# Moving the zero-point/scale table work and the weight-rebuild halves to other slots of an attention + GPTQ feed-forward kernel

## What is computed

```python
xn = layernorm(x)
# attention: 32 heads of 32, 8 key/value heads, rope, causal softmax
s = softmax(mask(q @ k.T / sqrt(32))) @ v @ wo
# feed-forward with 4-bit weights in groups of 128 rows
w_gu[i, f] = scale_gu[g[i], f] * (nibble_gu[i, f] - (zero_gu[g[i], f] + 1))     # 1024 x 5504
h = silu(xn @ w_gu[:, :2752]) * (xn @ w_gu[:, 2752:])
w_d[f, n] = scale_d[g[f], n] * (nibble_d[f, n] - (zero_d[g[f], n] + 1))         # 2752 x 1024
out = x + s * silu(h @ w_d)
```

## Time and profile before

| | us |
|---|---|
| median of 3 runs | 2474.61 (2474.33 to 2475.61) |
| the profiled execution | 2473.97 |
| its span, first to last instruction | 2472.2 |
| attention steps of the span | about 355 to 1550 |
| PE busy | 2338.2 (95%) |
| DVE busy | 1315.3 (53%) |
| POOL busy | 1162.1 (47%) |
| ACT busy | 890.5 (36%) |

### The profile page before, as it was taken

How to read it: one execution, slowest core, us unless ns; L and a number is a source line. 1 busy time by engine, 2 the same in 40 slices (tenths; PEclk the granted TensorE clock), 3 DMA queues, 4 the chain that set the end, 5 groups by cost and what they waited for, 6 DMA issues and landing times. The chain is left out here.

```text
span 2472.2 us, 41329 instructions
## 1 busy us (share of the span) xinstructions
PE 2338.2 (95%) x16296; PEld 1190.3 (48%) x16296; DVE 1315.3 (53%) x2164; ACT 890.5 (36%) x1665; POOL 1162.1 (47%) x1260
## 2 busy tenths in 40 slices
PE   6899969999999999999999999999969999999999
PEld 3555525555555555555555555444434444444443
DVE  4687467677777677777767775456331111111100
ACT  3222125555556555556555556222210101010100
POOL 2554327777777777777777777333201000101000
PEclk9999969999999999999999999999989999999999
DMA  5332301122221222221222212233182213222120
GB/s 162 99 94 67 86 18 39 45 74 52 68 63 55 60 55 70 68 59 54 66 52 68 69 47 56 75 102 93 48 306 95 77 62 109 84 87 99 55 80 17
DMA packets 229106, 187.62 MB, mean 76 GB/s; under 512 B 121617, under 2 KB 200954, under 8 KB 228544
## 3 DMA queue, kind: packets, MB, share of 16 engines
q1 hardware_dynamic: 228928, 185.21, 25.4%
HBM read 113.17 MB, written 71.86 MB: 75 GB/s over the span
## 5 line engine op out<-in xcount | busy, mean ns | idle before, releaser
L1046 PE MATMUL gu_ps<-xT,wg 128*128 128x512 f16 x4128 | 998.8, 382 | 1.7 <-ACT h L1119 1.7
L1292 POOL TENSOR_TENSOR room<-room 128x1152 f16<-128x1152 f32 x256 | 539.8, 2108 | 65.4 <-ACT room L1078 63.2
L1046 PEld LDWEIGHTS gu_ps<-xT,wg 128*128 128x128 f16 x4128 | 370.1, 98 | 390.7 <-issue 15.4
L1078 ACT ACTIVATE room<-sc_ps 128x512 f32<-128x512 f32 (+3 forms) x768 | 349.4, 489 | 512.8 <-PE sc_ps L971 511.9
L1683 POOL TENSOR_TENSOR room<-room 128x512 f32<-128x512 f32 x32 | 52.8, 1654 | 617.5 <-DVE room L1644 617.5
L1498 PE MATMUL dn_ps<-xT,hT_in 128*128 128x512 f16 x1536 | 337.2, 380 | 0.0
L1166 DVE TENSOR_REDUCE shift<-mx_ps 128x2 f16<-128x1024 f32 (+2 forms) x252 | 208.9, 829 | 147.9 <-PE mx_ps L953 143.9
L1644 DVE TENSOR_TENSOR room<-room 128x512 f32<-128x512 f32 x32 | 24.0, 754 | 428.6 <-ACT room L1572 428.6
L1287 POOL TENSOR_SCALAR_AFFINE_SELECT room<-room 128x128 f32<-128x128 f32 x512 | 153.0, 304 | 183.4 <-ACT room L1078 179.2
L1498 PEld LDWEIGHTS dn_ps<-xT,hT_in 128*128 128x128 f16 x1536 | 148.7, 98 | 181.6 <-issue 7.5
L949 PE MATMUL mx_ps<-arena 96*128 96x512 f16 x756 | 191.4, 335 | 38.8 <-DVE part L1166 33.4
(11 more groups left out here) (120 smaller groups left out, 3000.1 us busy)
## 6 DMA issues: line engine op xcount, KB each, us to landing
hidden_scratch<-hT SPq DMA_DIRECT2D x84, 256.0 KB, 3.0
hT_in<-hidden_scratch SPq DMA_DIRECT2D x16, 1344.0 KB, 5.9
o_scratch<-room SPq DMA_DIRECT2D x16, 1040.0 KB, 6.1
room<-o_scratch SPq DMA_DIRECT2D x16, 1040.0 KB, 8.2
arena<-q_scratch SPq DMA_DIRECT2D x48, 256.0 KB, 3.7
stock<-in_qw_d SPq DMA_DIRECT2D x42, 256.0 KB
down_scratch<-wd SPq DMA_DIRECT2D x84, 128.0 KB, 2.8
xin<-in_x SPq DMA_DIRECT2D x16, 512.0 KB, 4.1
```

The source lines that it names most:

```text
L1046: last = pe.matmul(to[:, :], wg[:, u, wp, s, cols], xT[:, xp, s, tokens], start=(s == 0 and k == 0), stop=(s == KT - 1 and k == 2))
L1078: act.activation(probs[:, r % 2, START[t] + c:START[t] + e], sc_ps[n % SC_BANKS][:, 0:e - c], ACT.Exp, scale=float(1.0 / np.sqrt(HD))).the ...
L1292: pool.tensor_tensor(p_lo[:, r % 2, c], probs[:, r % 2, c], p_hi[:, r % 2, c], ALU.subtract).then_inc(lo_done, 1)
```

## The change

It changes five things:

- The half rounds trade slots: gate/up from 1 and 5 to 3 and 7, down from 3 and 7 to 1 and 5.
- `select`: its four operations are spread over slots 3 and 7 of T0 and slots 3 and 7 of T1.
- The table of tile j + 2: the scaling (L140) and the two copies (L145, L146) go from VectorE to ScalarE (slot 3 of T1, slot 1 of T2). VectorE keeps the rest (slot 7 of T1), the low part (slot 3 of T2) and the zeros.
- The zeros are unpacked by one `bitwise_and` with broadcast masks (slot 7 of T2) in place of eight shifts, and turned to bfloat16 by one multiply with powers of 1/16 (slot 3 of T3) in place of a cast. Each has two SBUF inputs.
- `lanes` gets 16 more columns for the masks and the powers; `zn` has another shape.

```diff
@@ -670,9 +670,9 @@
 
 def half_rounds(t):
 
-    halves = [(1, "g", 2 * t), (5, "g", 2 * t + 1)]
+    halves = [(3, "g", 2 * t), (7, "g", 2 * t + 1)]
     if t >= 2:
-        halves += [(3, "d", 2 * t - 4), (7, "d", 2 * t - 3)]
+        halves += [(1, "d", 2 * t - 4), (5, "d", 2 * t - 3)]
     return sorted(halves)
...
@@ -1128,6 +1128,29 @@
                     act.wait_ge(ht_stored[q], 16 * (R // 2 * m + r // 2))
                 act.activation(hT[0:wt, q, 0, :], h[0:wt, q, :], ACT.Copy).then_inc(hhi_done, 1)
 
+            def table_scales(j, u):
+                w, first = tile_width(j), TABLE * (D_TABLES + j)
+                act.wait_ge(gu_loaded[u], 80 * (j // 2 + 1))
+                act.wait_ge(table_step, first)
+                act.activation(szt[:, u, 0, :, 0:w], scw[:, u, :, 0:w], ACT.Copy, scale=W_SCALE).then_inc(table_step, 1)
+
+            def table_parts(j, u):
+                w, first = tile_width(j), TABLE * (D_TABLES + j)
+                act.wait_ge(table_step, first + 2)
+                act.activation(mid[64:R_GU, :, 0:w], rest[64:R_GU, :, 0:w], ACT.Copy).then_inc(table_step, 1)
+                act.activation(szt[32:64, u, 0, :, 0:w], rest[32:64, :, 0:w], ACT.Copy).then_inc(table_step, 1)
+
+            def tables(m, r, at_slot):
+
+                if not unit(m, r):
+                    return
+                j, u, t = unit(m, r)
+                if j + 2 < FTILES:
+                    if (t, at_slot) == (1, 3):
+                        table_scales(j + 2, u)
+                    if (t, at_slot) == (2, 1):
+                        table_parts(j + 2, u)
+
             def wo_high(m, r):
 
                 if not isinstance(m, int) or not 0 <= R * m + r - (HELD - 3) < KT:
...
@@ -1199,35 +1223,77 @@
                 dve.scalar_tensor_tensor(wf[rows, p, cols], dif[rows, cols], 1.0, sz_ps[rows, 0, cols],
                                          ALU.subtract, ALU.mult).then_inc(wf_done, 1)
 
-            def select(m, r):
-
-                if not unit(m, r) or unit(m, r)[2] != 1:
-                    return
-                j, u, _ = unit(m, r)
+            def select(m, r, at_slot):
+
+                if not unit(m, r):
+                    return
+                j, u, t = unit(m, r)
                 wt = tile_width(j)
-                dve.wait_ge(idx_loaded, 16 * (j + 1))
-                dve.tensor_scalar(idf[:, 0, 0:wt], idx[:, 0:wt], 0.0, float(G_D), ALU.is_lt, ALU.mult
-                                  ).then_inc(sel_step, 1)
-                dve.wait_ge(sel_step, 3 * j + 1)
-                dve.tensor_tensor(idf[:, 1, 0:wt], idf[:, 0, 0:wt], idx[:, 0:wt], ALU.add).then_inc(sel_step, 1)
-                dve.wait_ge(sel_step, 3 * j + 2)
-                dve.tensor_scalar(idf[:, 0, 0:wt], idf[:, 1, 0:wt], 0.0, float(G_D - 1), ALU.max, ALU.min
-                                  ).then_inc(sel_step, 1)
-                dve.wait_ge(sel_step, 3 * j + 3)
-                dve.tensor_scalar(sel[:, u, 0:wt], idf[:, 0, 0:wt], lanes[0:R_D, 0:1], None, ALU.is_equal
-                                  ).then_inc(sel_done, 1)
-
-            def next_table(m, r, at_slot):
-
-                if not unit(m, r) or at_slot not in (3, 6):
-                    return
+                if (t, at_slot) == (0, 3):
+                    dve.wait_ge(idx_loaded, 16 * (j + 1))
+                    dve.tensor_scalar(idf[:, 0, 0:wt], idx[:, 0:wt], 0.0, float(G_D), ALU.is_lt, ALU.mult
+                                      ).then_inc(sel_step, 1)
+                if (t, at_slot) == (0, 7):
+                    dve.wait_ge(sel_step, 3 * j + 1)
+                    dve.tensor_tensor(idf[:, 1, 0:wt], idf[:, 0, 0:wt], idx[:, 0:wt], ALU.add).then_inc(sel_step, 1)
+                if (t, at_slot) == (1, 3):
+                    dve.wait_ge(sel_step, 3 * j + 2)
+                    dve.tensor_scalar(idf[:, 0, 0:wt], idf[:, 1, 0:wt], 0.0, float(G_D - 1), ALU.max, ALU.min
+                                      ).then_inc(sel_step, 1)
+                if (t, at_slot) == (1, 7):
+                    dve.wait_ge(sel_step, 3 * j + 3)
+                    dve.tensor_scalar(sel[:, u, 0:wt], idf[:, 0, 0:wt], lanes[0:R_D, 0:1], None, ALU.is_equal
+                                      ).then_inc(sel_done, 1)
+
+            def table_of(m, r):
+
+                if not unit(m, r):
+                    return None
                 j, u, t = unit(m, r)
-                if t < 2 or (isinstance(j, int) and j + 2 >= FTILES):
-                    return
-                piece = 2 * (t - 2) + at_slot // 6
-                if piece == 0:
-                    dve.wait_ge(gu_loaded[u], 80 * ((j - u) // 2 + 2))
-                gate_up_table(dve, table_step, TABLE * (D_TABLES + j + 2), piece, scw, zw, szt, rest, mid, zn, j + 2, u)
+                return (j + 2, u, t) if j + 2 < FTILES else None
+
+            def table_rest(j, u):
+                w, first = tile_width(j), TABLE * (D_TABLES + j)
+                dve.wait_ge(table_step, first + 1)
+                dve.scalar_tensor_tensor(rest[:, :, 0:w], scw[:, u, :, 0:w], W_SCALE, szt[:, u, 0, :, 0:w],
+                                         ALU.mult, ALU.subtract).then_inc(table_step, 1)
+
+            def table_low(j, u):
+                w, first = tile_width(j), TABLE * (D_TABLES + j)
+                dve.wait_ge(table_step, first + 4)
+                dve.tensor_tensor(szt[64:R_GU, u, 0, :, 0:w], rest[64:R_GU, :, 0:w], mid[64:R_GU, :, 0:w],
+                                  ALU.subtract).then_inc(table_step, 1)
+
+            def table_picks(j, u):
+                w, first = tile_width(j), TABLE * (D_TABLES + j)
+                half = w // NIB
+                dve.wait_ge(table_step, first + 5)
+                dve.tensor_tensor(zn[:, :, 0:half, :],
+                                  zw[0:G_GU, u, :, 0:half].unsqueeze(3).to_broadcast([G_GU, 2, half, NIB]),
+                                  lanes[0:G_GU, 2:2 + NIB].bitcast(U32).unsqueeze(1).unsqueeze(1).to_broadcast(
+                                      [G_GU, 2, half, NIB]), ALU.bitwise_and).then_inc(table_step, 1)
+
+            def table_zeros(j, u):
+                w, first = tile_width(j), TABLE * (D_TABLES + j)
+                half = w // NIB
+                dve.wait_ge(table_step, first + 6)
+                dve.tensor_tensor(szt[0:G_GU, u, 1, :, 0:w].rearrange("g h (c k) -> g h c k", k=NIB),
+                                  zn[:, :, 0:half, :],
+                                  lanes[0:G_GU, 2 + NIB:2 + 2 * NIB].bitcast(F32).unsqueeze(1).unsqueeze(1).to_broadcast(
+                                      [G_GU, 2, half, NIB]), ALU.mult).then_inc(table_step, 1)
+
+            def tables(m, r, at_slot):
+                if not table_of(m, r):
+                    return
+                j, u, t = table_of(m, r)
+                if (t, at_slot) == (1, 7):
+                    table_rest(j, u)
+                if (t, at_slot) == (2, 3):
+                    table_low(j, u)
+                if (t, at_slot) == (2, 7):
+                    table_picks(j, u)
+                if (t, at_slot) == (3, 3):
+                    table_zeros(j, u)
 
             def gated(m, r):
                 if not unit(m, r):
...
@@ -1261,9 +1327,8 @@
                     for slot, kind, n, j, u, number, p in halves(m, r):
                         if slot == i:
                             rebuild(kind, n, j, u, number, p)
-                    if i == 2:
-                        select(m, r)
-                    next_table(m, r, i)
+                    select(m, r, i)
+                    tables(m, r, i)
                 wo_low(m, r)
 
             dve.memset(shift[:, :, :, :], 0.0).then_inc(shift_set, 1)
...
@@ -1795,8 +1860,11 @@
 
 def lane_table():
 
-    p = np.arange(P)
-    return np.stack([p % 32, 4 * (p % NIB)], axis=1).astype(np.int32)
+    p, k = np.arange(P), np.arange(NIB)
+    lanes = np.stack([p % 32, 4 * (p % NIB)], axis=1).astype(np.int32)
+    picks = np.broadcast_to(np.left_shift(np.uint32(15), (4 * k).astype(np.uint32)).view(np.int32), (P, NIB))
+    shares = np.broadcast_to((16.0 ** -k).astype(np.float32).view(np.int32), (P, NIB))
+    return np.ascontiguousarray(np.concatenate([lanes, picks, shares], axis=1))
 
 
 def kernel(L0_attn_x, L0_attn_wq, L0_attn_wk, L0_attn_wv, L0_attn_wo, L0_ffn_qweight_gu, L0_ffn_qzeros_gu,
```

More of the change, by code:

```diff
@@ L162, in gate_up_table @@
     build_table(dve, step, first, part, scw[:, u, :, 0:w], szt[:, u, 0, :, 0:w], rest[:, :, 0:w], mid[:, :, 0:w],
-                zw[0:G_GU, u, :, 0:w // NIB], zn[:, :, 0:w].rearrange("g h (c k) -> g h c k", k=NIB),
+                zw[0:G_GU, u, :, 0:w // NIB], zn[:, :, 0:w // NIB, :],
                 szt[0:G_GU, u, 1, :, 0:w])
@@ L711, in attend_and_expand @@
     HELD = (NH // R + 1) * R
-    R_D = 64 + G_D
+    R_GU, R_D = 64 + G_GU, 64 + G_D
     D_TABLES = D // BANK
@@ L1200, in rebuild @@
                                          ALU.subtract, ALU.mult).then_inc(wf_done, 1)
```

(33 more changed lines are left out.)

## The result

The changed kernel takes **2485.8 us** (median of 5 runs, 2484.8 to 2486.9) against 2474.6 for the kernel before, measured beside it (5 runs, 2474.3 to 2479.1): ratio 1.0041, 95% interval 1.0026 to 1.0055. It is 11 us slower. The forecast was 2461 and faster; the range held the time, the sign was wrong.

What follows compares the result with a forecast made beforehand. TensorE, busy 95%, bounds it; only its waits and lower clock can be won. 70.3 + 1.2 (slots 3) + 1.2 (T3) + 1.5 (T2) = 74.2 us a tile against 75.1, over 15 tiles: about 2461 us, range 2428 to 2487.

Steps and rivals of the forecast that it cites:

- The floor, 70.3 a tile: The four attention steps of a tile without waits or clock loss: 2 x 17.35 + 2 x 17.8 us.
- T0's burst and the clock: VectorE's burst of work ahead of T0 goes, with its 2.1 us of waits and 1.3 of clock a tile.
- ScalarE's copies at nothing: Three table copies moved to ScalarE, at most 0.42 us each, were costed at nothing.
- Slots 3, 0.3 in each step: One more VectorE operation in slot 3 is blocked and delays slot 4's reduce: 0.3 us a step, 1.2 a tile.
- Slot 7: Extra VectorE operations at the step's end meet GpSimd's fourth subtraction: T3 waits 1.2 us, T2 1.5, T1 0.
- T0's race: Slot 7 of T0, extra against GpSimd's subtraction, starts within 0.1 us: T1 waits 0, or 1.7 if lost.
- Slots 3 and 7, the half round: Half rounds in slots 3 and 7 bring no new wait, TensorE's gate/up half being ready in time: cost nothing.
- a wait of TensorE for ScalarE as a sign of being wrong: The prediction called itself wrong if TensorE waits for ScalarE in slots 2 or 4; no size given.
- races lost: T0's slot 7 extra is blocked, T1 waits 1.7 us: 75.9 a tile, 2487 us; slower by this or clock 0.24.

Runs made afterwards that it cites:

- a_tabpre: The changed kernel with half rounds back in their old slots and, in slots 3 and 7, table and select operations ahead of the half round: 2402.6 us.
- a_both: The changed kernel with SyncE's down store ahead of its hidden-tile store, and table and select operations ahead of the half round in slots 3 and 7: 2403.1 us.
- a_tab: The changed kernel with the half rounds back in their old slots: 2427.6 us.
- a_dve: The changed kernel with the half rounds back in their old slots and the three table copies back on VectorE, same steps and slots: 2442.6 us.
- a_sp2: The changed kernel with SyncE's store of the down half ahead of its store of the hidden tile: 2454.9 us.
- a_pre: The changed kernel with VectorE's table and select operations in slots 3 and 7 ahead of the half round: 2437.7 us.
- b_pre: The kernel before with VectorE's select and table operations ahead of the half round of the same slot: 2476.0 us.
- a_lose: The changed kernel with the third select operation moved from slot 3 of T1 to slot 7 of T0: 2481.8 us.
- b_half: The kernel before with only the half rounds moved to their new slots: 2530.4 us.

## Why the prediction was wrong

By its own steps:

- **The floor, 70.3 a tile: right.** a_tabpre has 70.26, a_both 70.36.
- **T0's burst and the clock: right for the fifteen tiles.** T0 took 17.7 by the prediction and 17.62 measured, with a clock of 1.00, and no T3 has a lower one either. The fall at 1552 behind ScalarE's wait was not foreseen.
- **ScalarE's copies at nothing: right.** TensorE waits for ScalarE no more than 1.7 us in all in a_tab or a_tabpre, where ScalarE has the copies. Having them off VectorE is worth 15 us there (a_dve), for which the prediction named no price of its own.
- **Slots 3, 0.3 in each step: right for T0 and T1** (17.62 against 17.35 to 17.44 without). It is so in T2 too: 19.46 less 17.78 and less the 1.34 of slot 1 leaves 0.34, of which 0.15 shows as a wait. In T3 it is hidden by the late ScalarE.
- **Slot 7: right in all three places, in one of them by luck.** `table_rest` and `bitwise_and` were blocked. The prediction called T0's race closer than its rows could settle and took it as won; it was won in fourteen of fifteen tiles, in the one shown by 0.09. The sizes were 0.1 to 0.2 too large: T2's first maxima matmul came 1.34 us late (forecast 1.5), T3's 1.02 (1.2).
- **"Slots 3 and 7, the half round. [...] no new wait comes of it. [...] Nothing": this is the step that failed.** It looked at slots 3 and 7 and at TensorE's need for the half, and did not follow the half that was moved: the down half into slots 1 and 5, its ScalarE part, the buffer, the store, and SyncE's queue, on which the store stands behind a wait for another tensor. That is 1.75 us in each T3 (20.54 against 17.78 without waits, less 1.02 for the late reduce; a_sp2 takes away 1.52 of it, a_pre leaves 1.78) and 5 us in the end part. The run a_sp2 puts the whole at 31 us. The prediction had named a wait of TensorE for ScalarE as a sign of being wrong, but in slots 2 or 4 and with the three copies as its cause.

Put in the sum: 74.2 forecast, less 0.35 for the two sizes that were too large, less 0.3 for T3's hidden slot 3, plus 1.75, gives 75.3 against the 75.25 of the windows. In time: 75.49 less 74.2 is 1.3 a tile, 19 us over fifteen, and 5 in the end part; 2461 plus 24 is 2485, measured 2485.8. The rival that ended on the slower side (races lost, 2487) gave the number by a mechanism that occurred in one tile of fifteen.

The same step hid a second cost that the sum did have, but under another name. In a_tab the extras of slot 7 of T0 and T1 follow no half round and are in time; it is the gate/up half in slot 7 that puts them at GpSimd's subtraction. The changed kernel less a_sp2's 31 is still 27 us over a_tab: T2 19.47 against 18.11, T0 and T1 0.3 each, 1.9 x 15 = 29. **Of the 58 us that the trade costs in the changed kernel, 31 are SyncE's and 27 VectorE's, in operations that come behind GpSimd's subtractions.** With both repairs it costs nothing (a_both, a_tabpre).

The Trainium skill (SBUF — State Buffer, "Who interferes with whom") has it that the first to issue takes the shared pair for a whole instruction. The rows shown agree, down to a lead of 0.07 (b_pre) for GpSimd and 0.08 for VectorE (a_lose), and the part of the forecast that rested on it held. The Trainium skill (DMA: Bandwidth & Descriptors, "Anatomy of one DMA — SWDGE (gpsimd) path") also says that a wait for a semaphore is made on the issuing sequencer before dispatch. SyncE's rows here agree in kind: the down store is issued at 875.34, 0.68 behind the hidden one, though its data were complete at 859.15. Had I weighed this against the moved half, the cost could have been in the sum.

## What to carry to other kernels

Follow a moved step through everything it issues: its part on each engine, the buffer that it writes again, the store that frees the buffer, and what stands ahead of that store on its queue. Order the waits of a queue that serves two producers by when they are ready; trading two lines was worth 31 us here and nothing in the kernel where nobody waited. Where VectorE and GpSimd work on SBUF at the same time, an operation such as `table_rest` costs 0.4 or 2.3 us according to who starts first, so a plan for VectorE must be read against the start times of GpSimd's long instructions after every edit; an order that helps in one step may put the next operation in the same place.

## What was not expected of the hardware

- Two late engines partly hide each other. T3 takes 20.54 in the changed kernel, 19.02 with SyncE's order mended, 19.57 with VectorE's, 17.79 with both: 1.5 and 1.0 apart, 2.75 together.
- The one that comes second pays for the rest of the other's instruction, and a little more by its form: a blocked L1258 ended 0.28 after GpSimd (846.41 + 2.33 against 846.32 + 2.14), a blocked L1241 0.07 after it (826.04 + 2.01 against 825.83 + 2.15). For most operations this is what they take unblocked, less 0.13: L1258 0.41, L1241 0.22 and L1238 0.28 (blocked, it ends 0.15 after GpSimd). GpSimd's subtraction shows the other side in a small way: 2.11 alone, 2.14 and 2.15 where a VectorE operation of 0.28 leads it, 2.30 where L1258 leads it by 0.08 (a_lose).
- In the thirteen traces 1977 operations of VectorE on SBUF alone start well inside one of GpSimd's subtractions and end behind it, and eight do not. Four of the eight meet a subtraction that itself took 2.45 to 2.51. The other four start 0.005 to 0.013 behind, where the recorded starts no longer tell: others recorded 0.003 to 0.015 behind were blocked.
- The clock does not follow from the length of a wait by anything that the runs show. It never fell in a T3 of the changed kernel, where the longest wait was 1.72 (21.69 us, clock 1.00); it fell in one T3 of b_half behind a single wait of 1.69 (21.23 us, clock 0.92), in one T3 of a_lose behind 1.88 (22.46 us, clock 0.92), and in b_half in eleven of fifteen T0 steps behind a wait of 2.66, with 2.67 in three of the four others. What tells these apart no run here shows.
